# Scaling the expert weights by 64 on GpSimd instead of VectorE in a fused attention and mixture-of-experts kernel, with input rows in 512 KB transfers

## The reference, cut to what matters

```python
x = x + tanh(g_xattn[0]) * attention(layernorm(x), ctx_512, ctx_512)   # 32 query heads of 16, 8 key/value heads
x = x + tanh(g_ffn[0]) * moe(layernorm(x))

def moe(x):                        # 7 routed experts, 2 of them for a token, and one shared expert; all 512 x 512 x 512
    gate = x @ Wr + br
    ids = top_k(gate + gate_bias, 2)
    probs = softmax(gate at ids, -inf elsewhere)
    u = x @ Wup + bup              # for every expert
    g = silu(u @ Wgate + bgate) * u
    out = sum over experts of probs * (g @ Wdown + bdown)
    return out + the same with the shared weights Wsu, Wsg, Wsd
```

## Time and profile before

| | us |
|---|---|
| median of 3 runs | 1272.61 |
| lowest and highest run | 1270.43, 1278.21 |
| span of the profiled execution | 1271.7 |

### The profile page before, as it was taken

One profiled execution on the slowest core, in us unless ns is written; L12 is line 12 of the kernel. 1 busy time (PEld: TensorE's weight loads), 2 busy tenths in 40 slices (PEclk: granted clock), 3 DMA queues, 4 the chain that ended last, 5 costly groups with the idle time before them and its releaser, 6 DMA issues.

```text
span 1271.7 us, 40424 instructions
## 1 busy us (share of the span) xinstructions
PE 1197.0 (94%) x15162; PEld 889.3 (70%) x15162; DVE 852.9 (67%) x1470; ACT 585.5 (46%) x1131; POOL 382.3 (30%) x454
## 2 busy tenths in 40 slices
PE   3878889999878999999999999999999999999998
PEld 2544444555467777778888888888888888877775
DVE  5889989999887789445554455444444444447899
ACT  2767779898797422233333333333333333322221
POOL 4466766676830000210111111111111111006752
PEclk9888999999989999999999999999999999999999
DMA  5675555656665132644322454215412233057875
GB/s 183 211 247 176 176 172 187 212 186 212 209 252 190 52 133 67 225 152 152 119 82 82 139 183 157 66 58 193 146 66 66 66 125 123 33 175 234 265 227 176
DMA packets 91043, 196.32 MB, mean 154 GB/s; under 512 B 12128, under 2 KB 12640, under 8 KB 90976
## 3 DMA queue, kind: packets, MB, share of 16 engines
q1 hardware_dynamic: 80256, 160.30, 36.8%
q0 software_dynamic: 10720, 35.14, 9.2%
HBM read 331.68 MB, written 64.49 MB: 312 GB/s over the span
## 4 chain that ended last, share of the span: by engine, by line
PE 73%; DVE 12%; issue 5%; POOL 3%; DMA 3%; ACT 2%; SPq 1%; DVEq 1%; ACTq 0%; POOLq 0%
PE PS L1671 40%; PE PS L1709 20%; DVE negm L1011 5%; PE PS L1632 3%; PE PS L1484 3%; DMA qB<-negT 2%; PE PS L1518 2%; PE PS L1504 1%; ACT x2n L881 1%; POOL whl L696 1%; PE PS L1532 1%; DMA wr<-in_wr 1%; PE PS L1526 1%; DVE X L1314 1%; DVE rec L1024 1%
## 5 line engine op out<-in xcount | busy, mean ns | idle before, releaser
L1671 PE MATMUL PS<-xT,wb 128*128 128x128 f16 (+1 forms) x4128 | 279.8, 229 | 2.3 <-DVE gate L1152 1.6
L1671 PE MATMUL PS<-uhl,wb 128*128 128x128 f16 (+1 forms) x4128 | 279.8, 229 | 1.2 <-DVE uhl L1265 1.2
L1671 PEld LDWEIGHTS PS<-xT,wb 128*128 128x128 f16 x4128 | 264.1, 98 | 11.2 <-DVE gate L1152 1.7
L1671 PEld LDWEIGHTS PS<-uhl,wb 128*128 128x128 f16 x4128 | 263.5, 98 | 10.1 <-DVE uhl L1265 1.4
L1709 PE MATMUL PS<-wb,ghl 128*128 128x512 f16 x1200 | 267.2, 379 | 0.0
L1709 PEld LDWEIGHTS PS<-wb,ghl 128*128 128x128 f16 x1200 | 115.9, 98 | 130.2
L926 ACT ACTIVATE sl<-PS,bb 128x128 f32<-128x128 f32 (+1 forms) x344 | 106.7, 387 | 187.5 <-PE PS L1671 187.5
L747 POOL COPY ixr<-idx 128x2 int32 (+1 forms) x35 | 6.4, 183 | 593.3 <-PE PS L1632 593.3
L916 ACT ACTIVATE u<-PS,bb 128x128 f32<-128x128 f32 (+1 forms) x344 | 106.6, 387 | 169.5 <-PE PS L1671 164.1
L1272 DVE TENSOR_TENSOR g<-sl,u 128x512 f32<-128x512 f32 x102 | 70.5, 691 | 150.2 <-ACT sl L926 150.1
L1011 DVE TENSOR_REDUCE negm<-PS 128x8 f16<-128x1024 f32 x128 | 155.2, 1213 | 23.8 <-PE PS L1484 23.0
(11 more groups left out here) (161 smaller groups left out, 1375.9 us busy)
## 6 DMA issues: line engine op xcount, KB each, us to landing
wb<-wsc SPq DMA_DIRECT2D x219, 1024.0 KB
wst<-in_wall SPq DMA_DIRECT2D x32, 768.0 KB, 6.0
wsc<-whl SPq DMA_DIRECT2D x32, 768.0 KB, 4.3
ysl<-yb SPq DMA_DIRECT2D x43, 512.0 KB
bd<-in_bdown SPq DMA_DIRECT2D x74, 256.0 KB
X<-in_x SPq DMA_DIRECT2D x8, 1024.0 KB, 6.7
qB<-qT SPq DMA_DIRECT2D x32, 256.0 KB, 2.7
xnd<-xhl SPq DMA_DIRECT2D x32, 256.0 KB, 2.0
```

What stands on the lines that cost most here:

```text
L1671: ins = pe.matmul(bank_of(bank, t, m, kind), wb[:, j, l, k, w, m * P:(m + 1) * P], rhs(x, k)[:, ts], start=(n == 0), stop=(n == len(TERMS) ...
```

## The change

The multiplication by 64 moves from VectorE to GpSimd. On VectorE it stood in each body between `norm1` and the maxima for block b+2; on GpSimd it stands in each body right behind the residual of block b-1 and ahead of `rstd1`. It still runs in all 32 bodies. The rows of X come in 16 transfers of two blocks (512 KB) instead of 8 of four blocks (1 MB), one in each of the first bodies, and the context in three pieces (4, 10 and 18 blocks) instead of two (4 and 28).

```diff
+XP = NB // 2
+KEPT_C = (0, 4, 14, NB)
...
             def load_rows(cs):
                 for c in cs:
-                    sp.dma_start(X[:, c * n:(c + 1) * n, :], xv[:, c * n:(c + 1) * n, :]).then_inc(x_in[c], 16)
-            load_rows([0])
-            sp.dma_start(C[:, 0:n, :], ctxv[:, 0:n, :]).then_inc(c_in[0], 16)
-            load_rows([1])
+                    sp.dma_start(X[:, 2 * c:2 * c + 2, :], xv[:, 2 * c:2 * c + 2, :]).then_inc(x_in[c], 16)
+
+            def load_ctx(c):
+                sp.dma_start(C[:, KEPT_C[c]:KEPT_C[c + 1], :], ctxv[:, KEPT_C[c]:KEPT_C[c + 1], :]).then_inc(c_in[c], 16)
+            load_rows([0, 1])
+            load_ctx(0)
+            load_rows([2, 3])
...
-                if isinstance(half, int) and number(half, par) + 3 < XC:
-                    load_rows([number(half, par) + 3])
+                if isinstance(half, int) and number(half, par) + 5 < XP:
+                    load_rows([number(half, par) + 5])
+                if isinstance(half, int) and number(half, par) == 5:
+                    load_ctx(2)
...
+            def weights64(half, par):
+                g.wait_ge(w_in[par], 16 * (half + 1))
+                if not isinstance(half, int):
+                    g.nop(nofuse=True)
+                g.tensor_scalar(wst[:, par, :, :], wst[:, par, :, :], WS, None, ALU.mult).then_inc(S["w64_ready"], 1)
...
                 if not start:
                     residual(*pv)
+                weights64(half, par)
                 if late_chunk(half, par) is not None and par == 1:
                     rstd1(late_chunk(half, par)[0])
...
-            def weights64(half, par):
-                v.wait_ge(w_in[par], 16 * (half + 1))
-                v.tensor_scalar(wst[:, par, :, :], wst[:, par, :, :], WS, None, ALU.mult).then_inc(S["w64_ready"], 1)
...
-                weights64(half, par)
```

More of the change, by code:

```diff
@@ L201, in program @@
         qB_in = [sem(f"qB_in{j}") for j in range(2)]
-        x_in = [sem(f"x_in{c}") for c in range(XC)]
-        c_in = [sem(f"c_in{c}") for c in range(2)]
+        x_in = [sem(f"x_in{c}") for c in range(XP)]
+        c_in = [sem(f"c_in{c}") for c in range(3)]
         w_in = [sem(f"w_in{j}") for j in range(2)]
@@ L335, in _ @@
             xv = a["x"].rearrange("b p d -> p b d")
-            n = NB // XC
             ctxv = a["ctx"].rearrange("b t d -> t b d")
@@ L351, in _ @@
             load_w(1, 1)
-            load_rows([2])
+            load_rows([4])
             def queries_again(half, par, quad):
@@ L384, in _ @@
             neg_rows(0, 0, 1)
-            sp.dma_start(C[:, n:NB, :], ctxv[:, n:NB, :]).then_inc(c_in[1], 16)
+            load_ctx(1)
             def load_layer(l, e, j, cond):
@@ L725, in body @@
                     residual(*pv)
+                weights64(half, par)
                 if late_chunk(half, par) is not None and par == 1:
                     rstd1(late_chunk(half, par)[0])
-                if isinstance(half, int) and number(half, par) == 1:
-                    g.wait_ge(c_in[1], 16)
+                for c in (1, 2):
+                    if isinstance(half, int) and number(half, par) == KEPT_C[c] - 3:
+                        g.wait_ge(c_in[c], 16)
             over_batches(g, body)
@@ L851, in body @@
                 exps(half, par, 0)
-                if isinstance(half, int) and number(half, par) == 1:
-                    act.wait_ge(c_in[1], 16)
+                for c in (1, 2):
+                    if isinstance(half, int) and number(half, par) == KEPT_C[c] - 3:
+                        act.wait_ge(c_in[c], 16)
                 if later is not None:
@@ L960, in stats1 @@
             def stats1(c):
-                v.wait_ge(x_in[c], 16)
+                for pair in range(2 * c, 2 * c + 2):
+                    v.wait_ge(x_in[pair], 16)
                 for b in range(c * n, (c + 1) * n):
@@ L969, in late_stats1 @@
             def late_stats1(c, pair, one):
-                if pair == 0 and one == 0:
-                    v.wait_ge(x_in[c], 16)
+                if one == 0:
+                    v.wait_ge(x_in[2 * c + pair], 16)
                 b = c * n + 2 * pair + one
```

## The result

| | before | after |
|---|---|---|
| median | 1271.52 us (4 runs) | 1482.11 us (4 runs) |
| span of the profiled execution | 1271.7 us | 1479.4 us |

The change makes the kernel 1.163 times as long, interval 1.1594 to 1.1666. The forecast was 1415 us, the range 1355 to 1478: right in direction and mechanism, but 67 us too low and outside the range.

The account below looks back on a forecast made before the run. A closed chain of waits through GpSimd's multiplication was to bound attention: 13.6 us plus 1.35 for the lower clock, 14.95 a pass. Over 30 passes +144.1: 1271.7 + 144.1 - 2 + 0.9 = 1414.7, said as 1415; range 1355 to 1478 us.

Parts of the forecast that it names:

- The ring: Attention loop: closed chain of waits from one block's first exponential to the next's, 13.6 us a block against 9.23.
- the cost D of the multiplication: GpSimd's multiplication behind the residual: taken as 1.5 us, from short copies, between bounds of 0.95 and 3.11 us.
- The clock: TensorE in each attention pass: lower clock after idle time costs 0 to 2.8 us a block, 1.35 taken.
- the gap: TensorE in each pass: no work until the next block's first exponential is over, about 4 us.
- The stretch from the first exponential to the last transpose: Within each attention pass: kept at 8.33 us, as in the kernel before.
- The hand-overs: Waits between engines in each pass: 0.19 us from att to residual, 0.11 us from multiplication to conversion.
- The end: Blocks 29 and 30 of attention: fewer transposes and no warm-up work, -2 us.
- Transfers at 0: 512 KB row transfers: their gain is hidden by longer passes, 0; without the chain up to 9 us.
- The rival of the slow multiplication: GpSimd's multiplication at the speed of a two-input operation, 3.1 us: 1463 us, chance 0.11.
- The one that kept the clock up: TensorE in the loop: outputs and first scores fill enough of the gap, pass 13.6 us: 1374 us, chance 0.24.
- the one of no loss: Attention loop: conversion does not hold the next block, residual done before the fourth exponential: about 1235 us, chance 0.03.
- the one with the whole body at the lower clock: TensorE at the lower level all through each pass, 16.4 us: 1458 us, chance 0.13.

Follow-up runs that it names:

- the run with 24 matmuls: The changed kernel with 24 matmuls of 512 columns, results unread, filling TensorE's wait behind the previous block's outputs: 1456.64 us (one run).

## Why the prediction failed

*The mechanism was right.* The ring through conversion, exponentials, last transpose, att, residual and multiplication is what the timeline shows. Early and steady passes are alike, as forecast (16.6 to 17.3 us from conversion to conversion, blocks 2 to 30), and the multiplication ahead of the residual gives most of the loss back.

*The step that failed is the cost D of the multiplication*: "From above: no more than the subtraction of the same shape with two inputs, 3.11 us", of which 1.5 was taken. It takes 4.085 us. The bound rested on the thought that one input can't cost more than two; the row was of another operation. The copy's rate (1.463 us measured) says nothing of a product. The Trainium skill (GPSIMD Engine Reference, section 3.1) leads to estimates of 1.3 and 2.3 us; the measurement is above both. D alone is 2.58 us of a pass, 77 us in 30 passes and so more than the whole miss; the smaller terms below took some back. Why a constant costs GpSimd more than a second tensor stays open.

*The clock was sized right, in part by luck.* 1.35 us was taken, as about half of 0 to 2.8, and 1.38 is what the filled gap shows. But the gap was forecast at about 4 us and is 7.2. The Trainium skill (TensorE: Matmul & The Clock Gate, section on HAM oscillation) has a loop with a gap in each round pay each time; the trace agrees, with 0.50 in 344 to 352 us and 1.00 in 352 to 356, and a mean of 0.70 over 60 to 400.

*Smaller terms.* The stretch from the first exponential to the last transpose was kept at 8.33 us; it is 9.33 with the lower clock, where 8.33 + 1.35 = 9.68 was forecast. At full clock it is 7.86 in the run with 24 matmuls (284.43 to 292.29 us), so 8.33 was 0.47 too long (VectorE has one operation less there, which may be why; no run shows it), and the clock costs 1.47 of this stretch. The hand-overs came out 0.12 shorter. With D that makes 14.95 + 2.58 - 0.35 - 0.12 = 17.06 in the loop, and 16.95 in the mean.

*The end* was taken as -2 us and is +4.4: the last residual starts 14.9 us behind block 31's first exponential (563.70 - 548.78), against 11.3 before (356.77 us, told with the time before, less 345.45). It waits for att. The last transposes end 1.3 us later after that exponential than before, at a clock of 0.50 in 548 to 556 us. Then VectorE spends 3.27 us on an operation of the next stage (xhl), beside the last multiplication (0.68 at 571.14, where GpSimd is idle), and att comes another 2.3 us later. The remaining 0.8 us come behind that residual.

```profile
559.66 3.27 DVE L1124 TENSOR_TENSOR xhl<-x2n,xhl 128x512 f16<-128x512 f32 x1
```

```profile
559.18 4.08 POOL L703 TENSOR_SCALAR wst<-wst 128x1536 f32<-128x1536 f32 x1
563.70 1.64 POOL L697 TENSOR_TENSOR X<-X,att 128x512 f32<-128x512 f32 x1 [0.44 <-DVE att L1044]
```

Together: 30 x 2.00 for the passes is 60 us, the end 6.4; the start and what lies around the span nearly cancel: 66 us, the miss of the profiled execution (1481.14 us).

*Transfers at 0*: right to within 3 us; with the old ones the time is 1479.30. That they give up to 9 us without the ring was wrong as they stand (ratio 0.9991), because the third context piece brought a new wait of 4.43 us and a spell at the lower clock (0.50 in 104 to 108 us). With that piece cut up they give 0.4%.

*The rival of the slow multiplication* came nearest (1463 us), still with D too small. The one that kept the clock up and the one of no loss are refuted; the one with the whole body at the lower clock is not borne out, as the clock is 1.00 in 352 to 356 us.

## What to carry to other kernels

Before work is moved to an idle engine, draw the ring of waits that its new place closes: an operation behind the last link of a pass costs its full length in every pass, and an in-order engine makes such rings through everything that it lists behind it. Look also at what runs beside the operation at its new place. Bound an unseen cost only by the same operation on the same engine; a row of another operation is a guess at either end, and the range has to say so.

## What the runs showed of the hardware

- GpSimd's multiplication of 128x1536 float32 by a constant takes 4085 ns, 2.66 ns for an element of a row; the product with a second tensor, read over that shape, 3418, the subtraction to float16 3109, the copy 1463 ns. The number of inputs does not set the cost: of the two forms with one tensor, one is the cheapest and the other the dearest of the four.
- 96 small transposes more in each body of the loop doubled the instruction traffic (0.69 to 1.43 MB), and at the loop's jump back TensorE stood for up to 7.3 us on nothing but issue; the same columns in 24 matmuls did not do so.
- VectorE's xn, 128x512 float32, takes 527 ns in the mean with the change and 2054 with the multiplication moved ahead of the residual; at 298.48 us it ran 3.74 us, to just behind the end of GpSimd's multiplication.
- One transfer of 18 context blocks held up the next issue on its queue by 5.00 us; in pieces of three blocks the issue behind took 0.49 us.
